# Attention loop with two message tiles and two banks of sums, and each step's sums in two halves

## What is computed

```python
h = (x @ W).reshape(n, HEADS, OUT_C)
a1 = jnp.sum(h * attn_l, axis=-1)
a2 = jnp.sum(h * attn_r, axis=-1)
e = jax.nn.leaky_relu(a1[src] + a2[dst], negative_slope=0.2)
seg_max = jax.ops.segment_max(e, dst, num_segments=n)
ex = jnp.exp(e - seg_max[dst])
denom = jax.ops.segment_sum(ex, dst, num_segments=n)
alpha = ex / denom[dst]
out = jax.ops.segment_sum(h[src] * alpha[:, :, None], dst, num_segments=n)
```

## Time and profile before

| | us |
|---|---|
| median of 3 runs (8313.86 to 8317.8) | 8314.66 |
| profiled execution, its own time | 8320.46 |
| its span | 8318.7 |
| PE busy | 6649.0 (80%) |
| DVE busy | 4163.2 (50%) |
| POOL busy | 3454.7 (42%) |
| attention loop | about 870 to 3650 |
| relations loop | about 5650 to 7710 |

### The profile page before, as it was taken

How to read it: one execution, slowest core, us unless ns; L and a number is a source line. 1 busy time by engine, 2 the same in 40 slices (tenths; PEclk the granted TensorE clock), 3 DMA queues, 4 the chain that set the end, 5 groups by cost and what they waited for, 6 DMA issues and landing times. The chain is left out here.

```text
span 8318.7 us, 112232 instructions
## 1 busy us (share of the span) xinstructions
PE 6649.0 (80%) x30827; PEld 5064.5 (61%) x30828; DVE 4163.2 (50%) x8329; ACT 1094.1 (13%) x2687; POOL 3454.7 (42%) x3656
## 2 busy tenths in 40 slices
PE   1676799999999999965981999977888888888494
PEld 1555677777777777754650444445766776667363
DVE  3311566666666666663236111136655555555443
ACT  0244000000000000012430222220000000000131
POOL 0000555555555555514031000005777777777233
PEclk9977688888888888866995999998888888888597
DMA  5000333323333332332231222212333333333244
GB/s 164 30 2 31 85 82 84 86 81 82 87 82 83 85 85 81 83 103 81 77 92 40 110 102 106 106 63 79 105 105 105 105 105 105 105 105 104 71 133 125
DMA packets 323308, 737.78 MB, mean 89 GB/s; under 512 B 86054, under 2 KB 188232, under 8 KB 309896
## 3 DMA queue, kind: packets, MB, share of 16 engines
q0 software_dynamic: 174720, 490.64, 21.0%
q1 hardware_dynamic: 148488, 246.18, 8.3%
HBM read 555.75 MB, written 195.47 MB: 90 GB/s over the span
## 5 line engine op out<-in xcount | busy, mean ns | idle before, releaser
L824 POOL DMA_INDIRECT ga_ring<-h_dram,src_at x1624 | 1535.2, 945 | 2029.8 <-issue 1302.1
L824 POOL DMA_INDIRECT rg_ring<-y_dram,src_at x1624 | 1535.2, 945 | 1762.9 <-ACTq L1202 1268.5
L1054 PE MATMUL ga_psS<-ga_msg,ga_hot 128*128 128x280 f32 x4032 | 1493.0, 545 | 0.0
L1221 PE MATMUL rg_psS<-rg_ring,rg_hot_w 128*128 x4032 | 1163.8, 453 | 328.8 <-SPq L803 220.4
L1221 PEld LDWEIGHTS rg_psS<-rg_ring,rg_hot_w 128*128 128x128 f32 x4032 | 917.8, 232 | 585.2 <-issue 416.9
L1054 PEld LDWEIGHTS ga_psS<-ga_msg,ga_hot 128*128 128x128 f32 x4032 | 1053.0, 267 | 351.4
L1125 DVE SCALAR_TENSOR_TENSOR ga_hot<-ga_psN,pair_node,dstf 128x1024 f32<-128x1024 f32 x255 | 327.4, 1284 | 835.6 <-PE ga_psS L1054 833.2
L1411 PE MATMUL rr_psY<-rr_wr,rr_xt 128*128 128x512 f32 x1568 | 686.0, 596 | 0.0
L1137 DVE SCALAR_TENSOR_TENSOR ga_msg<-ga_psW,ga_ring 128x2112 f32<-128x2112 f32 x252 | 591.7, 2348 | 0.3 <-issue 0.3
L1032 PEld LDWEIGHTS ga_psX<-a,ga_hot_t 128*128 128x128 f32 x4064 | 501.3, 193 | 55.2 <-issue 19.0
L1411 PEld LDWEIGHTS rr_psY<-rr_wr,rr_xt 128*128 128x128 f32 x1568 | 294.5, 190 | 367.2 <-issue 367.2
(11 more groups left out here) (305 smaller groups left out, 7823.1 us busy)
## 6 DMA issues: line engine op xcount, KB each, us to landing
y_dram<-rr_y SPq DMA_DIRECT2D x98, 1024.0 KB, 3.9
f_x<-xg_dram SPq DMA_DIRECT2D x224, 128.0 KB, 2.1
yg_dram<-f_y SPq DMA_DIRECT2D x224, 128.0 KB, 1.7
ga_ring<-h_dram,src_at POOLq DMA_INDIRECT x1624, 2.8
rg_ring<-y_dram,src_at POOLq DMA_INDIRECT x1624, 2.7
xg_dram<-x SPq DMA_DIRECT2D x2, 6272.0 KB, 33.2
f_w<-L_ffn_W SPq DMA_DIRECT2D x16, 512.0 KB, 8.9
h_dram<-at_row SPq DMA_DIRECT2D x49, 136.0 KB, 1.8
```

Source lines behind the costliest of these rows:

```text
L824: p.indirect_dma_start(ring[:, (g % R) * G + j, :], None, table, bass.IndirectOffsetOnAxis(ap=rows[:, g * G + j:g * G + j + 1], axis=0)).t ...
L1054: o = pe.matmul(psS[:, 0:MROW], hot[:, u, j, :], msg[:, j, :], start=j == 0, stop=j == G - 1)
L1221: o = pe.matmul(psS[:, u % 2, 0:C], hot_w[:, u % 2, j, :], rows[:, j, :], start=j == 0, stop=j == G - 1)
```

## The change

`msg` becomes two tiles and `psS` two banks, taken in turn; `psW` goes into one bank for it. DVE makes the messages of pair t+1 in step t, after the scan, and takes `psS` of the other bank when it adds up. PE's sums of a pair are two halves, four of the eight matmuls at the start of the step and four at its end; the transposes of the scan and of `sta` stand one behind the other ahead of the second half, the scan's first. DVE now begins a step on `turned` (raised by the transpose of `sta`) of the step before, `back` is gone, and PE has one step more ahead of the loop. R goes from 6 to 7 and BASE from 5 to 6, for both loops that use them. LAG stays.

```diff
@@ -5,7 +5,7 @@
 
 P = 128
 G = 8
-R = 6
+R = 7
 LAG = 4
 GE = G * P
 C = 256
@@ -16,7 +16,7 @@
 NE = 8
 U = 4
 AHEAD = 3
-BASE = 5
+BASE = 6
 HW = D + 1
 HC1 = HEADS * HW
 HROW = HC1 + HEADS
@@ -952,23 +952,23 @@
         both = sb("both", [P, 2, 2, G + 1, HEADS])
         bent = sb("bent", [P, 2, G + 1, HEADS])
         arg = sb("arg", [P, 2, G + 1, HEADS])
-        msg = sb("msg", [P, G, MROW])
+        msg = sb("msg", [P, 2, G, MROW])
         psN = c.enter_context(nc.psum_tensor("ga_psN", [P, 512], F32))
-        psW = c.enter_context(nc.psum_tensor("ga_psW", [P, 2, 512], F32))
+        psW = c.enter_context(nc.psum_tensor("ga_psW", [P, 512], F32))
         psB = c.enter_context(nc.psum_tensor("ga_psB", [P, GE], F32))
         psI = c.enter_context(nc.psum_tensor("ga_psI", [P, 512], F32))
         psX = c.enter_context(nc.psum_tensor("ga_psX", [P, 512], F32))
-        psS = c.enter_context(nc.psum_tensor("ga_psS", [P, 512], F32))
+        psS = c.enter_context(nc.psum_tensor("ga_psS", [P, 2, 512], F32))
         gathered = [sem(f"gathered{s}") for s in range(R)]
         flagged = [sem(f"flagged{s}") for s in range(2)]
-        ready, room, go, pe_go, staged, turned, scanned, back, spread, spent, marked, maxed = (sem("m_" + x) for x in (
-            "ready", "room", "go", "pe_go", "staged", "turned", "scanned", "back", "spread", "spent", "marked", "maxed"))
+        ready, room, go, pe_go, staged, turned, scanned, spread, spent, marked = (sem("m_" + x) for x in (
+            "ready", "room", "go", "pe_go", "staged", "turned", "scanned", "spread", "spent", "marked"))
         shifts, args, weights, messages, summed = (
             sem(x) for x in ("shifts", "args", "weights", "messages", "summed"))
         psQ_v = psI[:, 2 * P:2 * P + GH].rearrange("p (j h) -> p j h", j=G)
         psX_v = psX[:, 0:GH].rearrange("p (j h) -> p j h", j=G)
         psL_v = psX[:, 2 * P:2 * P + G * A2].rearrange("p (j a) -> p j a", j=G)
-        w = psW[:, :, 0:(G + 1) * HEADS].rearrange("p u (j h) -> p u j h", j=G + 1)
+        w = psW[:, 0:2 * (G + 1) * HEADS].rearrange("p (u j h) -> p u j h", u=2, j=G + 1)
         iota = psN[:, 0:P].unsqueeze(1).to_broadcast([P, G, P])
         with nc.Block() as block:
             @block.vector
@@ -986,7 +986,7 @@
 
             @block.scalar
             def _(act):
-                act.sem_inc(weights, BASE - 1)
+                act.sem_inc(weights, BASE - 2)
 
                 def step(t, u, group):
                     early = isinstance(t, int)
@@ -1012,14 +1012,24 @@
 
             @block.tensor
             def _(pe):
-                pe.sem_inc(back, BASE - 4)
+                pe.sem_inc(turned, BASE - 5)
                 pe.sem_inc(summed, BASE)
                 pe.sem_inc(spread, BASE - 4)
+
+                def sum_up(t, u, part):
+                    for j in part:
+                        o = pe.matmul(psS[:, u % 2, 0:MROW], hot[:, u, j, :], msg[:, u % 2, j, :],
+                                      start=j == 0, stop=j == G - 1)
+                    return o
 
                 def step(t, u, group, block_no):
                     early = isinstance(t, int)
                     now = t + BASE if early else pe.snap(t + BASE)
-                    n2, n3 = (not early or t + q >= 0 for q in (2, 3))
+                    n0, n2, n3, n4 = (not early or t + q >= 0 for q in (0, 2, 3, 4))
+                    if n0:
+
+                        pe.wait_ge(messages, now)
+                        sum_up(t, u, range(0, G // 2))
                     if n3:
 
                         pe.wait_ge(spent, now)
@@ -1031,29 +1041,23 @@
                         for j in range(G):
                             pe.matmul(psL_v[:, j, :], hot_t[:, u % 2, j * P:(j + 1) * P],
                                       k.a12[:, ds(block_no(2) * A2, A2)], start=True, stop=True)
-
-                    if n3 and not n2:
+                    if n3:
+
                         pe.wait_ge(marked, now)
+                        for j in range(G):
+                            pe.matmul(psX_v[:, j, :], hot[:, (u + 3) % U, j, :], ends[:, j, :], start=True, stop=True)
+                    if n4:
+
+                        pe.wait_ge(scanned, now)
+                        pe.sem_inc(pe_go, 1)
+                        pe.transpose(psI[:, 2 * P:2 * P + GH], scan[:], k.ident[0:GH, 0:GH])
 
                     pe.wait_ge(staged, now)
                     pe.sem_inc(pe_go, 1)
                     pe.transpose(psI[0:GH, 0:P], sta[:].rearrange("p j h -> p (j h)"), k.ident[:]).then_inc(turned, 1)
-                    if n3:
-
-                        pe.wait_ge(marked, now)
-                        for j in range(G):
-                            pe.matmul(psX_v[:, j, :], hot[:, (u + 3) % U, j, :], ends[:, j, :], start=True, stop=True)
-
-                    pe.wait_ge(scanned, now)
-                    pe.sem_inc(pe_go, 1)
-                    pe.transpose(psI[:, 2 * P:2 * P + GH], scan[:], k.ident[0:GH, 0:GH]).then_inc(back, 1)
-                    if not early or t >= 0:
-
-                        pe.wait_ge(messages, now)
-                        for j in range(G):
-                            o = pe.matmul(psS[:, 0:MROW], hot[:, u, j, :], msg[:, j, :], start=j == 0, stop=j == G - 1)
-                        o.then_inc(summed, 1)
-                for t in range(-4, U):
+                    if n0:
+                        sum_up(t, u, range(G // 2, G)).then_inc(summed, 1)
+                for t in range(-5, U):
                     step(t, t % U, lambda d: one_of(pe, k.pair_group, max(t + d, 0), z.NGT - 1),
                          lambda d: one_of(pe, k.pair_block, max(t + d, 0), z.NB - 1))
                 with pe.Fori(1, z.T // U) as i, ExitStack() as held:
@@ -1066,11 +1070,12 @@
 
             @block.vector
             def _(v):
-                v.sem_inc(spent, BASE - 3)
                 v.sem_inc(shifts, BASE - 3)
                 v.sem_inc(marked, BASE - 4)
+                v.sem_inc(scanned, BASE - 5)
                 v.sem_inc(args, BASE - 2)
                 v.sem_inc(messages, BASE - 1)
+                v.sem_inc(spent, BASE - 3)
 
                 def fade(t, u, b):
 
@@ -1078,9 +1083,9 @@
                     v.tensor_tensor(heads, heads, w[:, u % 2, G, :].unsqueeze(2).to_broadcast([P, HEADS, HW]),
                                     ALU.mult)
 
-                def add_up(t, b):
+                def add_up(t, u, b):
                     rows = k.xb[:, ds(b * XW, MROW)]
-                    v.tensor_tensor(rows, rows, psS[:, 0:MROW], ALU.add)
+                    v.tensor_tensor(rows, rows, psS[:, u % 2, 0:MROW], ALU.add)
 
                 def step(t, u, group, block_no):
                     early = isinstance(t, int)
@@ -1090,9 +1095,9 @@
                     s1, s2 = (u + 1) % 2, u % 2
                     if n2:
                         tops = k.a12[:, ds(block_no(2) * A2, A2)]
+
+                    v.wait_ge(turned, now)
                     if n3:
-
-                        v.wait_ge(back, now)
                         v.tensor_tensor(ends[:], psQ_v, k.last[:, ds(group(3) * G, G)].unsqueeze(2).to_broadcast(
                             [P, G, HEADS]), ALU.mult)
                     if n1:
@@ -1126,23 +1131,21 @@
                             hot[:, (u + 3) % U, :, :], iota, k.pair_node[:, ds(t + 3, 1)],
                             k.dstf[:, ds(group(3) * G, G)].unsqueeze(2).to_broadcast([P, G, P]), ALU.add, ALU.is_equal
                         ).then_inc(marked, 1)
-                    if n0:
-                        if before:
-                            add_up(t - 1, block_no(-1))
-                        g = group(0)
-                        v.tensor_tensor(msg[:, :, HC1:], psN[:, 0:REL].unsqueeze(1).to_broadcast([P, G, REL]),
+                    v.tensor_tensor_scan(scan[:], flags[:, ds((group(4) % (2 * G)) * P, P)], psI[0:GH, 0:P], -BIG,
+                                         ALU.add, ALU.max).then_inc(scanned, 1)
+                    if before:
+                        add_up(t - 1, u + 1, block_no(-1))
+                    if n1:
+                        g = group(1)
+                        v.tensor_tensor(msg[:, s1, :, HC1:], psN[:, 0:REL].unsqueeze(1).to_broadcast([P, G, REL]),
                                         k.etf[:, ds(g * G, G)].unsqueeze(2).to_broadcast([P, G, REL]), ALU.is_equal)
 
                         v.wait_ge(weights, now)
                         v.scalar_tensor_tensor(
-                            msg[:, :, 0:HC1].rearrange("p j (h w) -> p j h w", w=HW),
-                            w[:, u % 2, 0:G, :].unsqueeze(3).to_broadcast([P, G, HEADS, HW]), MOST,
+                            msg[:, s1, :, 0:HC1].rearrange("p j (h w) -> p j h w", w=HW),
+                            w[:, s1, 0:G, :].unsqueeze(3).to_broadcast([P, G, HEADS, HW]), MOST,
                             ring[:, ds(slot(g), G), 0:HC1].rearrange("p j (h w) -> p j h w", w=HW),
```

(32 more changed lines are left out.)

## The result

The changed kernel took 7947.73 us (median of 4 runs, 7945.65 to 7948.51) where the one before took 8315.24 on the same chip: a ratio of 0.9557, 95% interval 0.9541 to 0.9574, 367.5 us less. The profiled execution took 7946.97 us with a span of 7944.8.

What follows compares the result with a forecast made beforehand. Bound: a PE-DVE circle of waits in the attention loop, plus clock falls. 8.2 + 1.27 = 9.45 us a step against 10.9, times 250, saves 362 us: 8320.5 to 7958, less 5.8 for the median, 7953 us; range 7850 to 8150.

Steps and rivals of the forecast that it cites:

- (a): Attention loop: with DVE scanning right behind `hot`, PE's wait of 0.82 us a step for the scan goes.
- (f): PE's clock in the attention loop: 0.75 stretches a step at the lower level, 1.27 us; range 0.5 to 1.2 stretches.
- (b): PE's new order in the attention loop: a step takes 8.2 us at the upper clock, with 0.07 for a change of kind.
- (c): New waits in the attention loop: DVE needs 7.65 us where PE needs 8.2, so DVE leaves the circle.
- (d): R = 7, one more slot in both loops' rings: worth nothing in the sum.
- (e): The attention loop's branch and two table loads, once in four steps: cost 0, with 0.25 us a step kept for the range.
- the clock at its upper level throughout (7640): Rival for the attention loop: the clock stays up, 8.2 us a step, gain 675 us, time 7640; chance 0.08.
- The clock as before (8152): Rival for the attention loop: the clock falls as often, 10.25 us a step, time 8152; chance 0.16 with its neighbours.

Runs made afterwards that it cites:

- scan_late_new: The changed kernel with DVE's scan put back behind the message; 7952.32 us, ratio 0.9553 to the kernel before.
- scan_early_old: The kernel before with only its scan moved up, between the one-hot tile and the adding of the sums; 8588.78 us, ratio 1.0319.
- whole_last: The changed kernel with all eight matmuls for the sums at the end of PE's step, behind the wait for the message; 7956.98 us, ratio 0.9547.
- whole_first: The changed kernel with all eight matmuls for the sums at the start of PE's step, not split; 8059.74 us, ratio 0.9671.
- between_5: The changed kernel with five sums matmuls first and three between the narrow matmuls of psL and psX; 7784.35 us, ratio 0.9338.
- between_4: The changed kernel with the second half of the sums moved between the narrow matmuls of psL and psX; 7786.88 us, ratio 0.9345.
- three_323: The changed kernel with the sums matmuls in three parts: 3 first, 2 between psL and psX, 3 last; 7967.39 us, ratio 0.9562.
- three_332: The changed kernel with the sums matmuls in three parts: 3 first, 3 between psL and psX, 2 last; 7697.19 us, ratio 0.9237.
- three_242: The changed kernel with the sums matmuls in three parts: 2 first, 4 between psL and psX, 2 last; 7750.02 us, ratio 0.9301.

## Why the prediction was right

The time, 7953 us against 7947.7, and most terms of the sum agree. The cause that it gave for (a) is half of the story, and the number in (f) was luck. One reading was wrong without harm: the row of the page that shows 7 in the attention loop is that of PEld; PE shows 9 there. The sum does not use it.

- **(a) the wait of 0.82 us goes.** It went. The prediction laid it to the scan's place right behind `hot`. `scan_late_new` shows that this place is worth nothing in the changed order, and `scan_early_old` that alone it costs 3.2%. What counts first is that no wide matmul waits for a message of its own step. The early scan would be needed if the sums were not in halves, by the estimate from `whole_last`; this was not run.
- **(b) 8.2 us at the upper clock.** Measured 8.10. The 0.07 added for a change of kind was not there (8.13 without it).
- **(c) DVE leaves the circle.** It did: it waits 0.9 us for `turned`, and for `summed` only in the steps with a stretch at the lower clock. PE waits for nothing. DVE's 7.65 us were right: where it waited for nothing, it took 7.63 from one `ends` to the next, with 0.47 to spare against 8.10:

```profile
2002.44 0.23 DVE L1101 TENSOR_TENSOR ga_ends<-ga_psI,last 128x64 f32<-128x64 f32 x1 [1.73 <-PE ga_psI L1057]
...
2010.07 0.23 DVE L1101 TENSOR_TENSOR ga_ends<-ga_psI,last 128x64 f32<-128x64 f32 x1
```

- **(d) the seventh slot, 0.** Held in both directions.
- **(e) the loop's loads, 0.** Held for the change, by the second half's cover, and this was the term nearest to being wrong: without that cover (`whole_first`) the loads cost 0.2 us a step and about as much again through the clock.
- **(f) 0.75 stretches of 1.7 us.** Measured 0.74 (135 of 182 steps) and 1.70. The cost of one was read from rows. The part without wide matmuls came out at 4.33 us (2005.42 to 2009.75), where the prediction had 4.2, with a 0.1 in it that no row gives. The number of stretches was a choice between 0.66 and 0.92, leaning on the idea that less standing means fewer falls. The later runs give that idea little: standing adds falls where it lengthens a narrow part (`between_5`), but the order moved the clock from 0.86 to 1.00 though it brought 51 us of standing with it (`between_4`). That the choice came out to a hundredth was good fortune: `three_323` against `three_332` shows how steep the dependence is, and a line between two loops could not have told it.

The sum: 10.9 - 9.38 = 1.52 us a step, and 367.5/1.52 = 242 steps' worth; the prediction had 1.45 and 250. The first steps, written out ahead of the loop, did not gain: from 870 to 960 us PE ran 313 matmul instructions in both kernels. The prediction's two errors, 0.07 us a step and some eight steps, offset each other in part.

Of the rivals, the clock at its upper level throughout (7640) is a matter of the order of the same instructions, as the later runs show: `three_332` comes near it with 7697. The clock as before (8152) came in no run; nearest is `whole_first`, with 8060 and falls in seven steps of eight. The Trainium skill, "TensorE: Matmul & The Clock Gate", in the section "HAM oscillation", lays a fall of the clock within a kernel to idle gaps. These rows speak against its use here: PE was busy for all of the 6.8 us before the falls at 2020.2 and 2030.5.

## What to carry to other kernels

When two engines wait for each other once in every step, find the one product that closes the circle and make it a step early. Moving another operation of the circle forward instead can cost time (3.2% here). Afterwards look at what the bound engine has queued where its loop branches and loads registers, and keep wide matmuls there. And lay wide matmuls between the narrow ones, since the order alone decided between a clock of 0.86 and one of 0.99, 3.5% of the time.

## What was not expected of the hardware

In a loop where PE never stands, the clock fell to its lower level in three steps of four, around the end of a part of 4.3 us without wide matmuls, in which 32 of the 36 instructions had 8 or 16 columns. The same instructions with wide matmuls in between gave a mean clock of 0.99 to 1.00 with eight of their instructions in the middle (`between_4`, `three_242`), 0.99 or 0.96 with six (`three_332`, `between_5`), and 0.86 with four (`three_323`). With six or more, the only falls came in the steps in which PE stood at the loop's loads. In the rows looked at, a stretch at the lower clock lasted 3.4 us or about twice that. PE's sequencer took 1.0 us for each of two table loads; a pause in PE from them shows only as idle time put down to "issue".
